# Linear attention of a two-layer decoder: the output projection as three products of parts, over two pairs of heads at a time

## The chip, the cores and the metric

The kernel runs on one core of a Trainium2 chip. The metric is the device time of one execution in microseconds, lower is better. Before the change three runs took 2131.28 to 2137.3 us, median 2136.52.

## The reference

The whole kernel is a decoder of two layers on x, 2 x 512 tokens of 512 features (1024 rows): mixer, cross attention, experts, then linear attention, gated cross attention and an MX feed-forward, each added to x after a layer norm. The change touches the fourth, linear attention (32 heads of 64 features, 16 pairs of heads):

```python
qkv = silu(h @ qkv_w.T)                       # h: normed x; q, k, v of 32 heads x 64
aw = einsum('bhid,bhjd->bhij', qi, ki) * dd   # per block, with decay
intra = einsum('bhij,bhjd->bhid', aw, vi)
inter = einsum('bhid,bhde->bhie', qi * qd_, state)
new_state = state * bd_ + einsum('bhsd,bhse->bhde', ki * kd_, vi)
attn = rmsnorm(intra + inter, norm_w)         # over all 2048 features
gate = sigmoid(h @ gate_w.T)
x = x + (gate * attn) @ out_w.T               # 1024 x 2048 by 2048 x 512
```

## The kernel before, in words

The stage is `linear_attention` (lines 1294 to 1799). Each engine has its own program, written out by hand; they meet only at semaphores, and every engine works strictly in its order. After the layer norm there is a loop over `PAIRS` = 16 pairs of heads, grouped by `GP` = 4. Tokens are 1024 in eight tiles of 128 (`TT`), in two halves of 512 (`BANK`); `CH` = 4 chunks of 128 per half.

**Parts.** An operand in F32 is split as high = rounded to F32R (ScalarE, a Copy) and low = operand - high (VectorE). `product_of_parts` (lines 227 to 231) multiplies high x high, high x low and low x high into one PSUM bank. The projections (weights `w3`, line 1457) and the values (`wv`, line 1477) go this way already. The output projection, `sum_outputs` (lines 1537 to 1546), is a plain F32 product, which the chip runs as two instructions.

**TensorE**, per pair p (lines 1551 to 1566): q.k products of the first half (line 1492), turning of the keys (1503), one projection of pair p + 1, q.k of the second half, three more projections, state updates (1513), two gate projections, outputs (1529 and 1533, PSUM banks 6 and 7). At the end of a group of four pairs come the values of the next group (eight tiles, banks 0 and 1) and then `sum_outputs(g)`: for each of eight token tiles four products, over the group's four pairs, into bank 2 or 3. These two banks are also those of q.k.

**ScalarE** (lines 1624 to 1637): moves the projections out of PSUM with Silu or Sigmoid (`pair(p + 1)`; a table load of 1.28 us stands between the two functions), makes the high parts of the weights (1611), squares the outputs (1604), at a group's end moves the values (1597); after the last pair it makes the high parts of four context tensors for the next stage (1637).

**VectorE** (lines 1780 to 1798): masks q.k (1707), decays the keys (1716), rounds the feed-forward's weights in units of two steps that have nothing to do with this stage (`round_weights`), makes low parts of weights (1767, 1772), computes the states S (1730, 1732), gates the outputs (`gate`, 1745: the normed weight times PSUM times the sigmoid, into `ga`), and at a group's end rounds two more units and adds the projection's tiles to y (`add_outputs`, 1760 and 1762). In the last one the low parts of the context tensors (1751) stand between the adds.

**GpSimd** (lines 1643 to 1659): per pair, decays the queries into `qD` (1650) and sums the squares (1659).

**SyncE** issues all transfers, also in a fixed order (lines 1407 to 1448): per pair the three projection weights, mask and query decay, stores of rounded feed-forward weights and reloads of the slot (`FSLOTS` = 4 slots in `fw`), every fourth pair the values' weights and the output weights `wo` of four pairs (1 MB). Before several of these it waits for the engine that frees the buffer.

`ga` holds five pairs (`GA`). The next stage starts after a barrier behind the last add.

## Time and profile before

| | us |
|---|---|
| median of three runs | 2136.52 |
| the profiled execution | 2135.23 |
| its span | 2133.4 |
| PE busy (share of the span) | 1935.3 (91%) |
| DVE / ACT / POOL busy | 1168.6 / 635.2 / 219.6 |
| the stage's loop in the span, about | 968 to 1576 |

PE is TensorE, DVE VectorE, ACT ScalarE, POOL GpSimd, SP SyncE; times in rows are microseconds from the span's start, unless ns. A row of the timeline has the start, the time it took, the engine, the line of the kernel, the operation, output <- inputs and how many instructions were merged; in brackets the idle time of that engine before it and what ended that. A matmul's own time includes its way through the array, so the distance between starts is what one costs. L229 to L231 are the three lines of `product_of_parts`.

### The profile page before, as it was taken

How to read it: one execution, taken by the hardware profiler on the slowest of the kernel's cores; microseconds unless marked ns; L12 is line 12 of the kernel's file. 1: busy time of each engine (PE TensorE's matmuls, PEld its weight loads, DVE VectorE, ACT ScalarE, POOL GpSimd, SP SyncE). 2: the span in 40 equal slices, each digit the busy share in tenths (PEclk: the TensorE clock that was granted, in tenths of full speed). 3: DMA queues.
4: the chain of work that ended last, by engine and by line, in shares of the span. 5: the costliest groups of instructions: out<-in, count | busy, mean ns of one | idle time of the engine just before them, and what ended most of it. 6: DMA issues, size and time to landing. Idle time of an engine off the chain costs nothing. (4 is left out here: it accounts for less than half of the span.)

```text
span 2133.4 us, 24875 instructions
## 1 busy us (share of the span) xinstructions
PE 1935.3 (91%) x9621; PEld 1409.3 (66%) x9624; DVE 1168.6 (55%) x2069; ACT 635.2 (30%) x1013; POOL 219.6 (10%) x185
## 2 busy tenths in 40 slices
PE   7899795899997599979999999999899998899996
PEld 6677783444433458847886886877758744688885
DVE  5412737555543345547674684665643378656653
ACT  3311322444444055514340331322224221222110
POOL 0000001111201100000120120210200001112221
PEclk9999896899998599999999999999999999999998
DMA  5100402222210500014221313203202100110101
GB/s 198 40 1 0 158 11 67 67 68 58 64 37 1 158 0 1 1 36 140 77 79 66 114 54 116 97 20 117 80 31 70 60 20 22 58 37 25 39 1 40
DMA packets 67125, 124.12 MB, mean 58 GB/s; under 512 B 8512, under 2 KB 26944, under 8 KB 65472
## 3 DMA queue, kind: packets, MB, share of 16 engines
q1 hardware_dynamic: 67008, 122.53, 18.1%
q8 instruction: 77, 1.26, 0.2%
q14 instruction: 40, 0.33, 0.0%
HBM read 88.82 MB, written 14.68 MB: 49 GB/s over the span
## 5 line engine op out<-in xcount | busy, mean ns | idle before, releaser
L941 DVE TENSOR_REDUCE b_nm<-ps 128x1 f32<-128x1024 f32 x128 | 151.5, 1220 | 118.8 <-PE ps L862 118.8
L929 ACT ACTIVATE b_pr<-ps 128x512 f32<-128x512 f32 x256 | 132.3, 605 | 159.5 <-PE ps L880 159.5
L229 PE MATMUL ps<-d_x_high,d_w_high 128*128 128x512 f32 x384 | 154.8, 403 | 4.4 <-DVE d_w_low L1767 4.4
L230 PE MATMUL ps<-d_x_low,d_w_high 128*128 128x512 f32 x384 | 150.4, 392 | 0.0
L231 PE MATMUL ps<-d_x_high,d_w_low 128*128 128x512 f32 x384 | 150.3, 392 | 0.0
L892 PE MATMUL ps<-b_pr,b_VS 128*64 128x512 f32 x512 | 130.6, 634 | 0.0
L1544 PE MATMUL ps<-d_wo,d_ga 128*128 128x512 f32 x256 | 110.6, 593 | 1.5 <-DVE d_ga L1745 1.5
L880 PE MATMUL ps<-b_qS,b_kS 98*128 98x512 f32 x256 | 92.3, 442 | 20.1 <-DMA b_qS<-b_nm_parts 17.7
L862 PE MATMUL ps<-b_kS,b_qS 96*128 96x512 f32 x256 | 95.0, 461 | 15.6 <-DMA b_qS<-b_q_parts 10.1
L880 PEld LDWEIGHTS ps<-b_qS,b_kS 98*128 98x128 f32 x256 | 44.1, 192 | 90.7 <-issue 52.1
L1659 POOL TENSOR_TENSOR d_sqsum<-d_sqsum,d_sq 128x512 f32<-128x512 f32 x32 | 42.4, 1325 | 487.4 <-ACT d_sq L1604 487.2
L1544 PEld LDWEIGHTS ps<-d_wo,d_ga 128*128 128x128 f32 x256 | 48.6, 190 | 61.3 <-issue 59.3
L229 PEld LDWEIGHTS ps<-d_x_high,d_w_high 128*128 128x128 f32 x384 | 72.5, 189 | 20.2 <-DVE d_w_low L1767 4.7
L231 PEld LDWEIGHTS ps<-d_x_high,d_w_low 128*128 128x128 f32 x384 | 72.5, 189 | 15.6
L230 PEld LDWEIGHTS ps<-d_x_low,d_w_high 128*128 128x128 f32 x384 | 72.7, 189 | 13.7
L862 PEld LDWEIGHTS ps<-b_kS,b_qS 96*128 96x128 f32 x256 | 53.4, 217 | 36.0 <-DVE b_nm L941 17.0
L892 PEld LDWEIGHTS ps<-b_pr,b_VS 128*64 128x64 f32 x512 | 32.9, 144 | 60.4 <-issue 51.8
L1228 DVE TENSOR_TENSOR c_hF<-ps,c_sq 128x512 f32<-128x512 f32 x64 | 44.3, 692 | 48.6 <-ACT c_sq L1216 48.6
L2333 ACT ACTIVATE f_hF_high<-ps 128x512 fp32r<-128x512 f32 x32 | 19.1, 598 | 158.2 <-PE ps L2220 158.2
L1707 DVE TENSOR_TENSOR d_A<-ps,d_mask 128x512 f32<-128x512 f32 x64 | 41.1, 684 | 36.1 <-issue 31.6
L93 POOL TENSOR_TENSOR rstd<-var_eps,neg_half 128x8 f32<-128x8 f32 x5 | 8.2, 1644 | 508.6 <-DVE var_eps L106 508.6
L1198 PEld LDWEIGHTS ps<-c_r2T,c_hF 128*128 128x128 f32 x512 | 59.5, 192 | 1.2
(372 smaller groups left out, 4592.5 us busy)
## 6 DMA issues: line engine op xcount, KB each, us to landing
b_kS<-b_k_parts SPq DMA_DIRECT2D x96, 128.0 KB, 2.3
f_rows<-d_fw SPq DMA_DIRECT2D x24, 512.0 KB, 3.0
f_w<-f_rows SPq DMA_DIRECT2D x12, 1024.0 KB, 4.8
b_qS<-b_q_parts SPq DMA_DIRECT2D x96, 64.0 KB, 2.0
a_convT<-in_convT SPq DMA_DIRECT2D x4, 1024.0 KB, 12.8
b_ctxT<-in_ctxT SPq DMA_DIRECT2D x8, 512.0 KB, 5.1
d_w<-in_d_wq SPq DMA_DIRECT2D x16, 256.0 KB, 4.4
d_w<-in_d_wk SPq DMA_DIRECT2D x16, 256.0 KB, 4.3
```

The lines of the kernel that those rows point to most:

```text
L229: nc.tensor.matmul(out, lhsT[0], rhs[0], start=start, stop=False)
L230: nc.tensor.matmul(out, lhsT[0], rhs[1], start=False, stop=False)
L231: return nc.tensor.matmul(out, lhsT[1], rhs[0], start=False, stop=stop)
L862: last = nc.tensor.matmul(c.ps[:, banks + n, :], qS[0:96, s_, h, t * P:(t + 1) * P], kS[0:96, s_, h, n * BANK:(n + 1) * BANK], start=True, ...
L880: nc.tensor.matmul(c.ps[:, 4 + n % BANKS, :], kS[0:98, g % 2, h, k * P:(k + 1) * P], qS[0:98, g % 2, h, :], start=True, stop=True).then_in ...
L892: last = nc.tensor.matmul(c.ps[2 * DH * hh:2 * DH * (hh + 1), 7, :], VS[:, 2 * (q % 2) + hh, k * VW:k * VW + VPAD], pr[:, (n + hh) % RING, :],
L929: nc.scalar.activation(pr[:, n % RING, :], c.ps[:, 4 + n % BANKS, :], ACT.Exp).then_inc(exp_done, 1)
L941: nc.vector.tensor_reduce(nm[:, g % 2, u:u + 1], c.ps[:, banks:banks + 2, :], AX.XY, ALU.max, negate=True).then_inc(job_read, 1)
L1198: last = nc.tensor.matmul(c.ps[:, 4 + n, i * LAT:(i + 1) * LAT], hF[:, e % 2, k, t * P:(t + 1) * P], r2T[:, e, k, :], start=k == 0, stop=k ...
L1228: nc.vector.tensor_tensor(hF[:, e % 2, m, n * BANK:(n + 1) * BANK], c.ps[:, 2 + j % 2, :], sq[:, j % 2, :], ALU.mult).then_inc(h_done, 1)
L1544: last = nc.tensor.matmul(c.ps[:, 2 + j % 2, :], ga[:, (g * GP + k) % GA, t * P:(t + 1) * P], wo[:, k, :], start=k == 0, stop=k == GP - 1)
L1659: nc.gpsimd.tensor_tensor(sqsum[:, tok], sqsum[:, tok], sq[:, b, :], ALU.add).then_inc(sqsum_done, 1)
```

## The change

The output projection is computed with `product_of_parts` from high and low parts of the gated outputs and of its weights. It is summed over two pairs (`SG` = 2, eight sums) instead of four. Sum i is done in the middle of pair 2i + 2, between that pair's second and third projection for the next pair, the last one at the end. ScalarE makes high parts of each pair's gated outputs after its squares and, every second pair, of the output weights (512 KB now, one buffer whose low part is written in place); VectorE makes the low parts between the key decay and the second mask product of the next pair, and adds the sum's tiles behind that mask product. SyncE loads output weights at every even round of its queue, after waiting for the sum two pairs back. `ga` shrinks to two pairs, its parts hold two, and the slots of the raw feed-forward weights go from four to three.

```diff
--- before.py
+++ after.py
@@ -1312,22 +1312,25 @@
     wv_parts = [take("wv_high", [P, KD, DM], F32R, 8), c.at("d_wv_low", [P, KD, DM], F32R, at - 16)]
     w3 = take("w3", [P, 3, KD, P], F32, 6)
     w3_parts = [take(f"w3_{part}", [P, 3, KD, P], F32R, 6) for part in ("high", "low")]
-    wo = take("wo", [P, GP, DM], F32, 8)
+    SG = 2
+    SUMS = PAIRS // SG
+    wo = take("wo", [P, SG, DM], F32, 4)
+    wo_parts = [take("wo_high", [P, SG, DM], F32R, 4), c.at("d_wo_low", [P, SG, DM], F32R, at - 8)]
     x_parts = [c.at("d_x_high", [P, KD, TOK], F32R, 16), take("x_low", [P, KD, TOK], F32R, 16)]
     v = take("v", [P, TT, DM], F32, 16)
     qF = take("qF", [P, TOK], F32, 4)
     qD = take("qD", [P, TOK], F32, 4)
     kF = take("kF", [P, TOK], F32, 4)
     kT = take("kT", [P, TT, P], F32, 4)
-    GA = GP + 1
-    ga = take("ga", [P, GA, TOK], F32, 4 * GA)
+    ga = take("ga", [P, 2, TOK], F32, 8)
+    ga_parts = [take(f"ga_{part}", [P, SG, TOK], F32R, 8) for part in ("high", "low")]
     A = take("A", [P, 2, 2, CH, P], F32, 8)
     S = take("S", [P, CH - 1, 2, P], F32, 3)
     sq = take("sq", [P, 2, BANK], F32, 4)
     sqsum = take("sqsum", [P, TOK], F32, 4)
-    FR, FSLOTS = 2, 4
+    FR, FSLOTS = 2, 3
     FUNITS = len(FJOBS) * KD // FR
-    fw = take("fw", [P, FSLOTS, FR * BANK], F32, 16)
+    fw = take("fw", [P, FSLOTS, FR * BANK], F32, 12)
     faux = take("faux", [P, FR * BANK], F32, 4)
     fscale = take("fscale", [P, FR * BANK // MX], F32, 0.125)
     finv = take("finv", [P, FR * BANK // MX], F32, 0.125)
@@ -1350,6 +1353,7 @@
     t_done, t_moved = c.sem("d_t_done"), c.sem("d_t_moved")
     u_done, s_ready = c.sem("d_u_done"), c.sem("d_s_ready")
     o_done, sq_done, ga_done = c.sem("d_o_done"), c.sem("d_sq_done"), c.sem("d_ga_done")
+    ga_high, ga_low, wo_high, wo_low = (c.sem(f"d_{n}") for n in ("ga_high", "ga_low", "wo_high", "wo_low"))
     qd_done, sqsum_done = c.sem("d_qd_done"), c.sem("d_sqsum_done")
     step, zeroed = c.sem("d_step"), c.sem("d_zeroed")
     in_cw, in_cx, c_high, c_low = (c.sem(f"d_{n}") for n in ("in_cw", "in_cx", "c_high", "c_low"))
@@ -1364,7 +1368,11 @@
 
     def a_jobs(p):
 
-        return 4 * p + TT * (p // GP)
+        return 4 * p + TT * (max(p - 1, 0) // SG)
+
+    def sum_job(i):
+
+        return 4 * min(SG * (i + 1) + 1, PAIRS) + TT * i
 
     def pair_weights(sp, p):
         for i, name in enumerate(("d_wq", "d_wk", "d_wg")):
@@ -1386,6 +1394,11 @@
     def units_rounded(p):
 
         return UNITS_FIRST + p + UNITS_GROUP * (p // GP) if p >= 0 else 0
+
+    def output_weights(sp, i):
+        if i >= 1:
+            sp.wait_ge(a_done, sum_job(i - 1) + TT)
+        sp.dma_start(wo[:], tiled(c.dram["d_woT"])[:, SG * i:SG * (i + 1), :]).then_inc(in_o, 16)
 
     def group_values(sp, g):
         sp.dma_start(wv[:], tiled(c.dram["d_wvT"])[:, :, g * DM:(g + 1) * DM]).then_inc(in_v, 16)
@@ -1407,6 +1420,8 @@
             for p in range(PAIRS):
                 if p >= 1:
                     pair_weights(sp, p)
+                if p % SG == 0 and p > SG:
+                    output_weights(sp, p // SG - 1)
                 if p >= 3:
                     sp.wait_ge(a_moved, a_jobs(p - 3) + 4)
                     sp.wait_ge(qd_done, 2 * (p - 2))
@@ -1427,11 +1442,8 @@
                         sp.wait_ge(proj_done, first_job(GP * (g - 1)) + 6 + TT)
                         group_values(sp, g)
                     if g == 0:
-                        sp.dma_start(wo[:], tiled(c.dram["d_woT"])[:, 0:GP, :]).then_inc(in_o, 16)
-                if p % GP == 1 and p > 1:
-                    g = p // GP
-                    sp.wait_ge(a_moved, a_jobs(GP * g))
-                    sp.dma_start(wo[:], tiled(c.dram["d_woT"])[:, g * GP:(g + 1) * GP, :]).then_inc(in_o, 16)
+                        output_weights(sp, 0)
+            output_weights(sp, SUMS - 1)
             sp.wait_ge(proj_done, first_job(PAIRS - 1) + 6)
             sp.dma_start(ctx.wkT[:], tiled(c.dram["e_wkT"])).then_inc(in_cw, 16)
             sp.dma_start(ctx.ctxT[:, 0], tiled(c.dram["ctxT"])[:, :, 0:CHUNK]).then_inc(in_cx, 16)
@@ -1534,15 +1546,16 @@
                                                     A[:, b, hh, ch, :], start=ch == 0, stop=True, skip_group_check=True)
                     last.then_inc(o_done, 1)
 
-            def sum_outputs(g):
-                pe.wait_ge(ga_done, 2 * GP * (g + 1))
-                pe.wait_ge(in_o, 16 * (g + 1))
+            def sum_outputs(i):
+                pe.wait_ge(wo_low, i + 1)
                 for t in range(TT):
-                    j = a_jobs(GP * (g + 1)) - TT + t
+                    j = sum_job(i) + t
+                    if t % CH == 0:
+                        pe.wait_ge(ga_low, 2 * (SG * (i + 1) - 1) + t // CH + 1)
                     pe.wait_ge(a_moved, j - 1)
-                    for k in range(GP):
-                        last = nc.tensor.matmul(c.ps[:, 2 + j % 2, :], ga[:, (g * GP + k) % GA, t * P:(t + 1) * P], wo[:, k, :],
-                                                start=k == 0, stop=k == GP - 1)
+                    for k in range(SG):
+                        last = product_of_parts(nc, c.ps[:, 2 + j % 2, :], [x[:, k, t * P:(t + 1) * P] for x in ga_parts],
+                                                [w[:, k, :] for w in wo_parts], k == 0, k == SG - 1)
                     last.then_inc(a_done, 1)
 
             queries_keys(0, 0, 4)
@@ -1555,15 +1568,18 @@
                     queries_keys(p + 1, 0, 1)
                 products(p, 1)
                 if p + 1 < PAIRS:
-                    queries_keys(p + 1, 1, 4)
+                    queries_keys(p + 1, 1, 2)
+                if p % SG == 0 and p > 0:
+                    sum_outputs(p // SG - 1)
+                if p + 1 < PAIRS:
+                    queries_keys(p + 1, 2, 4)
                 updates(p)
                 if p + 1 < PAIRS:
                     gates(p + 1)
                 outputs(p)
                 if p + 1 < PAIRS and (p + 1) % GP == 0:
                     values((p + 1) // GP)
-                if p % GP == GP - 1:
-                    sum_outputs(p // GP)
+            sum_outputs(SUMS - 1)
 
         @block.scalar
         def _(act):
@@ -1578,13 +1594,13 @@
                         act.wait_ge(qd_done, 2 * p)
                     if i == 2 and p >= 1:
                         act.wait_ge(t_done, 2 * p)
-                    if i == 4 and p >= GA:
-                        act.wait_ge(a_done, a_jobs(GP * ((p - GA) // GP + 1)))
+                    if i == 4 and p >= 2:
+                        act.wait_ge(ga_low, 2 * (p - 1))
                     if i < 4:
                         dst = (qF, kF)[i // 2][:, tok]
                         nc.scalar.activation(dst, src, ACT.Silu).then_inc(proj_moved, 1)
                     else:
-                        nc.scalar.activation(ga[:, p % GA, tok], src, ACT.Sigmoid).then_inc(proj_moved, 1)
+                        nc.scalar.activation(ga[:, p % 2, tok], src, ACT.Sigmoid).then_inc(proj_moved, 1)
                     if i % 2 == 1 and p + 1 < PAIRS:
                         high_weights(p + 1, i // 2)
 
@@ -1602,6 +1618,20 @@
                     if p >= 1:
                         act.wait_ge(sqsum_done, 2 * (p - 1) + b + 1)
                     nc.scalar.activation(sq[:, b, :], c.ps[:, 6 + b, :], ACT.Square).then_inc(sq_done, 1)
+
+            def high_gated(p):
+                for b in range(2):
+                    tok = slice(b * BANK, (b + 1) * BANK)
+                    act.wait_ge(ga_done, 2 * p + b + 1)
+                    if b == 0 and p >= SG:
+                        act.wait_ge(a_done, sum_job(p // SG - 1) + TT)
+                    nc.scalar.activation(ga_parts[0][:, p % SG, tok], ga[:, p % 2, tok], ACT.Copy).then_inc(ga_high, 1)
+
+            def high_outputs(i):
+                act.wait_ge(in_o, 16 * (i + 1))
+                if i >= 1:
+                    act.wait_ge(a_done, sum_job(i - 1) + TT)
+                nc.scalar.activation(wo_parts[0][:], wo[:], ACT.Copy).then_inc(wo_high, 1)
 
             def high_weights(p, i):
 
@@ -1625,6 +1655,9 @@
                 if p + 1 < PAIRS:
                     pair(p + 1)
                 squares(p)
+                high_gated(p)
+                if p % SG == SG - 1:
+                    high_outputs(p // SG)
                 if p % GP == GP - 2 and p + 2 < PAIRS:
                     high_values(p // GP + 1)
                 if p + 1 < PAIRS and (p + 1) % GP == 0:
@@ -1742,8 +1775,19 @@
                 for b in range(2):
                     tok = slice(b * BANK, (b + 1) * BANK)
                     dve.wait_ge(sq_done, 2 * p + b + 1)
-                    nc.vector.scalar_tensor_tensor(ga[:, p % GA, tok], c.ps[:, 6 + b, :], nw[:, p:p + 1],
-                                                   ga[:, p % GA, tok], ALU.mult, ALU.mult).then_inc(ga_done, 1)
+                    nc.vector.scalar_tensor_tensor(ga[:, p % 2, tok], c.ps[:, 6 + b, :], nw[:, p:p + 1],
+                                                   ga[:, p % 2, tok], ALU.mult, ALU.mult).then_inc(ga_done, 1)
+
+            def low_gated(p):
+                for b in range(2):
+                    tok = slice(b * BANK, (b + 1) * BANK)
+                    dve.wait_ge(ga_high, 2 * p + b + 1)
+                    nc.vector.tensor_tensor(ga_parts[1][:, p % SG, tok], ga[:, p % 2, tok],
+                                            ga_parts[0][:, p % SG, tok].bitcast(F32), ALU.subtract).then_inc(ga_low, 1)
+
+            def low_outputs(i):
+                dve.wait_ge(wo_high, i + 1)
+                nc.vector.tensor_tensor(wo_parts[1][:], wo[:], wo_parts[0][:].bitcast(F32), ALU.subtract).then_inc(wo_low, 1)
 
             def context_low(i):
                 loaded, count, raw, parts = c_splits[i]
@@ -1754,7 +1798,7 @@
                 for t in range(TT):
                     if between and t < len(c_splits):
                         between(t)
-                    j = a_jobs(GP * (g + 1)) - TT + t
+                    j = sum_job(g) + t
                     dve.wait_ge(a_done, j + 1)
                     if g == 0:
                         nc.vector.tensor_copy(y[:, t, :], c.ps[:, 2 + j % 2, :]).then_inc(a_moved, 1)
@@ -1780,7 +1824,13 @@
             for p in range(PAIRS):
                 mask_products(p, 0)
                 decay_keys(p)
+                if p % SG == 0 and p > 0:
+                    low_outputs(p // SG - 1)
+                if p >= 1:
+                    low_gated(p - 1)
                 mask_products(p, 1)
+                if p % SG == 0 and p > 0:
+                    add_outputs(p // SG - 1)
                 if p >= 1:
                     round_weights(1)
                 low_weights(p + 2, 0)
@@ -1792,10 +1842,11 @@
                     round_weights(1)
                 low_weights(p + 2, 2)
                 gate(p)
-                if p % GP == GP - 1:
-                    if p + 1 < PAIRS:
-                        round_weights(2 * UNITS_GROUP)
-                    add_outputs(p // GP, context_low if p + 1 == PAIRS else None)
+                if p % GP == GP - 1 and p + 1 < PAIRS:
+                    round_weights(2 * UNITS_GROUP)
+            low_outputs(SUMS - 1)
+            low_gated(PAIRS - 1)
+            add_outputs(SUMS - 1, context_low)
     c.rms = sqsum, ones, ms, y
 
 
```

## Rows read from the trace of the kernel before

**Rows 1.** The page's list of engines: busy us (share of the span) x instructions.

```profile
PE 1935.3 (91%) x9621; PEld 1409.3 (66%) x9624; DVE 1168.6 (55%) x2069; ACT 635.2 (30%) x1013; POOL 219.6 (10%) x185
```

**Rows 2.** Busy time by stretch: pair 14, then pair 15; granted clock, DMA share, GB/s last.

```profile
1503.10:1527.40 24.30, 24.30 (x182) 20.51 (x180) 15.02 (x32) 7.35 (x10) 5.00 (x5) 1.00 0.07 18
...
1527.40:1546.80 19.40, 10.42 (x112) 9.36 (x108) 12.80 (x26) 2.61 (x4) 6.36 (x6) 0.82 0.57 196
```

**Rows 3.** Waits of TensorE in the stage: total us, times, longest.

```profile
PE ps L1533 <- DVE d_S L1732: 6.9, 1, 6.9
...
PE ps L1492 <- DVE d_y L1762: 1.7, 2, 0.9
...
PE ps L1492 <- DVE d_y L1760: 0.9, 1, 0.9
```

**Rows 4.** Timeline of the tail, VectorE and TensorE.

```profile
1546.02 0.75 DVE L1745 SCALAR_TENSOR_TENSOR d_ga<-ps,d_nw,d_ga 128x512 f32<-128x512 f32 x1 [1.29 <-ACT d_sq L1604]
...
1546.82 27.73 PE L1544 MATMUL ps<-d_wo,d_ga 128*128 128x512 f32 x64 [1.49 <-DVE d_ga L1745]
...
1574.59 0.69 DVE L1762 TENSOR_TENSOR d_y<-ps,d_y 128x512 f32<-128x512 f32 x1 [2.74 <-PE ps L1544]
```

**Rows 5.** Timeline, first and last of 96 products of the values.

```profile
1108.28 0.50 PE L229 MATMUL ps<-d_wv_high,d_x_high 128*128 128x512 f32 x1
...
1129.99 0.39 PE L231 MATMUL ps<-d_wv_high,d_x_low 128*128 128x512 f32 x1
```

**Rows 6.** Groups by line and form: count, busy us, mean ns, idle before.

```profile
L1611 ACT ACTIVATE d_w_high<-d_w 128x512 fp32r<-128x512 f32 x48 | 29.7, 622 | 5.1 <-DMA d_w<-in_d_wq 3.2 <-PEq L194 1.9
...
L1637 ACT ACTIVATE e_ctx_high<-e_ctxT 128x1024 fp32r<-128x1024 f32 x2 | 2.1, 1046 | 0.0
...
L1751 DVE TENSOR_TENSOR e_wk_low<-e_wkT,e_wk_high 128x2048 fp32r<-128x2048 f32 x1 | 2.3, 2291 | 1.0 <-ACT e_wk_high L1637 1.0
...
L1751 DVE TENSOR_TENSOR e_ctx_low<-e_ctxT,e_ctx_high 128x1024 fp32r<-128x1024 f32 x2 | 2.4, 1215 | 0.0
```

**Rows 7.** Line 1767's durations in ns (min/median/max); GpSimd's timeline at a group's end.

```profile
L1767 DVE TENSOR_TENSOR d_w_low<-d_w,d_w_high x48: 680/692/1770, 969.3 to 1501.2; 128x512 fp32r<-128x512 f32 x48
...
1107.55 3.16 POOL L1659 TENSOR_TENSOR d_sqsum<-d_sqsum,d_sq 128x512 f32<-128x512 f32 x2 [19.04 <-ACT d_sq L1604]
```

**Rows 8.** Timeline of pair 14, three engines.

```profile
1503.13 1.16 PE L1492 MATMUL ps<-d_qF,d_kF 64*128 64x128 f32 x16
...
1508.00 1.16 PE L1492 MATMUL ps<-d_qF,d_kF 64*128 64x128 f32 x16
...
1517.39 1.50 PE L1513 MATMUL ps<-d_v,d_kT 128*128 128x128 f32 x12
...
1505.74 1.28 DVE L1716 TENSOR_TENSOR d_kT<-ps,d_kdec 128x512 f32<-128x512 f32 x2
...
1514.20 1.28 DVE L1979 TENSOR_TENSOR d_fw<-d_fw,d_fscale 128x512 f32<-128x512 f32 x2
...
1518.93 0.61 DVE L1730 COPY d_S<-ps 64x128 f32<-64x128 f32 x2 [3.44 <-PE ps L1513]
...
1519.64 1.56 DVE L1732 SCALAR_TENSOR_TENSOR d_S<-d_S,d_bdec,ps 64x128 f32<-64x128 f32 x4
...
1505.15 2.55 POOL L1650 TENSOR_TENSOR d_qD<-d_qF,d_qdec 128x512 f32<-128x512 f32 x2
```

**Rows 9.** Timeline at the first group's end, ScalarE and VectorE.

```profile
1111.42 1.28 ACT L1597 ACT_TABLE_LOAD   x1 [2.42 <-PE ps L231]
...
1109.58 1.41 DVE L1745 SCALAR_TENSOR_TENSOR d_ga<-ps,d_nw,d_ga 128x512 f32<-128x512 f32 x2
```

**Rows 10.** SyncE's timeline, and the page's list of DMA issues (median us to landing).

```profile
1161.94 0.43 SPq L1381 DMA_DIRECT2D f_rows<-d_fw  x1
...
1181.26 0.43 SPq L1373 DMA_DIRECT2D d_w<-in_d_wq  x1
...
d_w<-in_d_wq SPq DMA_DIRECT2D x16, 256.0 KB, 4.4
```

## The prediction

> **What bounds the kernel now.** I read the profile from the whole down to the one product that is changed. The page's list of engines comes first: TensorE is busy 91% of the span and the next engine 55% [rows 1]. The table by stretches then shows an ordinary pair of heads in this stage: 24.3 us, TensorE busy through all of it, VectorE 15 us, ScalarE 7 us, GpSimd 5 us, full clock [rows 2]. So in this stage time is the number of TensorE cycles, and any other engine has room as long as it is not late at one of the hand-overs. The second row there is the last pair, which has no projections of a next pair to fill its waits: 10.4 of 19.4 us. The list of waits names TensorE's idle time: 6.9 us for the state S in that last pair, and 2.6 us in three waits for the running sum y, once at the start of each later group [rows 3].
>
> The output projection is four blocks of 64 F32 instructions (32 products of two instructions each); one takes 27.7 us [rows 4], so a product costs 0.865 us. Three of the blocks stand after the values of the next group, the fourth is the stage's tail.
>
> **The change, part by part.**
> *Three products of parts.* The values have the same shapes (128x128 stationary, 512 columns) in F32R parts. Their 96 products start at 1108.28 and the last at 1129.99 [rows 5]: 21.71/95 = 0.2285 us from one to the next. Three are 0.686 us against 0.865. One sum over two pairs has 8 x 2 x 3 = 48 of them, 11.0 us. Seven such sums stand inside pairs: 76.8 us, say, against 3 x 27.7 = 83.1 us. **-6.3 us.** The eighth is in the tail.
>
> *Waits at the group start.* The F32 block was followed directly by the products q·k, whose banks waited for y [rows 3]. Now values are followed by q·k, whose banks have been free since the pair before. **-2.6 us.**
>
> *Added work on ScalarE and VectorE, each pair.* Two high copies of 128x512 (0.62 us each) and every second pair one of 128x1024 (1.05 us) on ScalarE; two subtractions of 128x512 (0.69 us) and every second pair one of 128x1024 (1.22 us) on VectorE [rows 6, 7]. y is added eight times per two pairs in place of eight per four, at 0.69 us [rows 4]. Altogether VectorE gets 32 x 0.69 + 8 x 1.22 + 32 x 0.69 = 54 us more. VectorE has 9 us free in a pair; the even pair also grows by 11.0 us, 8 x 0.69 = 5.5 of which are adds. By share nothing is lost; the order decides.
>
> *The even pair up to the sum.* Take pair 14 [rows 8]. TensorE starts q·k at 1503.13, the second half at 1508.00; that takes 1.16 us and one projection 2.74, so the sum would start at 1511.9. VectorE ends the key decay at 1507.02 and then has the subtraction of the weights, two of the gated values and the first mask product: 1.22 + 0.65 + 0.65 + 0.65. A subtraction with both inputs in SBUF that meets a GpSimd operation is late: 0.69 us usually, 1.77 once GpSimd's sum of squares had begun at 1107.55 [rows 7]. Here GpSimd multiplies queries until 1507.70, so 0.7 us more: 1510.9. Slack 1.0 us. **0**, covered by the projection between; without that cover each microsecond counts seven times.
> The Trainium skill (SBUF — State Buffer, Who interferes with whom) says that a VectorE instruction with two SBUF inputs contends with a GpSimd instruction that reads SBUF, and that the loser blocks for the other's whole instruction; the 1.77 us agrees. By that rule the change buys TensorE time with exactly the kind of instruction that GpSimd can hold up.
>
> *The even pair behind the sum.* VectorE's last add ends 0.9 us after the sum. Then come rounding (5 us), one weight subtraction (0.7) and the states (2.2), which may start when the updates are done, 2 x 2.74 + 1.5 = 7.0 us after the sum. They end at 9.2; TensorE's outputs start at 7.0 + 2 x 2.74 = 12.4. **0**, 3 us of slack. (In pair 14 rounding ends at 1515.48, 6.3 us after the second q·k, 1.3 of which are masks; the states take from 1518.93 to 1521.2, updates 1.5 us [rows 8].)
>
> *The group's end.* ScalarE waits there, after the squares, for the gated values, then copies both halves and the weights, and the first value's activation with its table load stands behind that. VectorE's gating starts at 1109.58 and ends at 1110.99 [rows 9]; copies of 0.65 and 1.0 us bring ScalarE to 1112.65, table load and activation (1.28 + 0.60) to 1114.55. The table load was at 1111.42 before. TensorE's third tile of values needs that bank at 1108.28 + 24 x 0.2285 = 1113.76. 0.9 us with the semaphore, three times. **+2.7 us.**
>
> *The last pair.* Nothing covers VectorE here, and two subtractions (1.35 us) stand ahead of the mask products and the states. As in pair 14, GpSimd's multiplications end 0.7 us after the key decay (1507.70 and 1507.02 [rows 8]): 0.7 more. **+2.05 us.**
>
> *The tail.* Before: the second gating from 1546.02 to 1546.77, the F32 block from 1546.82, the last add over at 1575.28 [rows 4]. After: gating, second high copy (1547.4), weights' high copy (1548.4), their subtraction (1549.65), first low half (1550.3): the sum starts 3.5 us later. It is 11.0 us of TensorE, but VectorE still has to subtract four context tensors between the first four adds (2 x 2.29 + 2 x 1.22 = 7.0 us [rows 6]), the second low half 0.65 and four adds 2.6: 1560.6. Only then may tile 5 run; 5, 6 and 7 take 4.1 us and the last add 0.85: 1565.4. **-9.9 us.** After some 5 us of idle TensorE the clock may be at its 1.2 GHz level, as it was in the first part of the last pair (0.82 on average there [rows 2]); mostly hidden behind VectorE: **+0.5 us.**
>
> *SyncE's queue.* The load of the output weights now waits, in every second round of the queue, for the sum two pairs back, and behind it stand masks, the stores and reloads of the rounded weights (three slots instead of four), the values' weights and the next pair's projection weights. Longest are the rounds with three stores: before, 19.3 us from the first store to the query weights [rows 10]. These transfers would start 1.5 us after the sum, and the query weights land 1.5 + 19.3 + 4.4 (median for this load [rows 10]) = 25.2 us after it. ScalarE asks for them after the second projection of the next pair, which is one pair's length behind the sum, 24.3 us. 0.9 us late, where TensorE's next need is 2 to 3 us further. With fewer transfers beside them than in that row they should be earlier. **0.** The third slot costs VectorE at most 1 to 2 us in three pairs, inside the 3 us of slack.
>
> **Sum:** -6.3 - 2.6 + 2.7 + 2.05 - 9.9 + 0.5 = -13.6 us. The profiled execution took 2135.2 us (span 2133.4), so 2121.7; the median of the runs is 1.3 us above it: **2123 us**.
>
> **Bounds of what the trace does not show.** The pitch of the new products: 0.2267 us (a steady stretch of projections) to 0.235: 0.7 us down, 2.5 up over the 384. The wait before a sum inside a pair: 0 to 1.4 us, the latter if all three subtractions take 1.77: 3 x 1.08 - 0.7 already counted, less 1.0 of slack, some 1.5; times seven, 10 us. I take 0, since GpSimd has nothing left to do after 1507.7. The tail: 11.0 + 1.5 us if nothing were in its way, 6 us less than my figure. The group's end: 0 (ScalarE's copies finding room) to 1.5 each.
>
> **The rivals.**
> 1. *TensorE's whole saving arrives* (32 x 4 x 0.18 = 23 us and the 2.6 us): the tail is not held by VectorE and the group ends cost nothing, about 2111. Against it: VectorE's 13 us of work in the tail are there whatever TensorE does. Chance 0.08.
> 2. *The low parts come late in the middle of pairs.* The port of GpSimd and VectorE holds each subtraction; 1.4 us at seven sums: -13.6 + 9.8, about 2133. For it: one such subtraction of 1.77 us is seen. Against: only the first of the three can meet GpSimd's multiplications. Chance 0.15. This is no change by measure.
> 3. *SyncE's queue becomes the bound, and the kernel slower.* Place: the projection weights of pairs 7, 11 and 15, behind three stores and three reloads. Up to 3 us late they cost nothing; beyond that TensorE stands with ScalarE, three times. If the chain took 10 us longer than the row shows, 7 or more each, over 20 us: about 2144. It decides from 6.7 us of stall each. For it: that queue already spends its time waiting, and one slot fewer ties each reload to a store that has just been issued. Against: the computed lateness is 0.9 us. Chance 0.06.
> 4. *The products of parts do not run at 0.23 us* because weights and values are written shortly before; at 0.29 us the saving is gone. Every product of parts in the trace has the same pitch. 0.02.
>
> Forecast, with its bounds (2116 to 2130): 0.69.
>
> **How the numbers follow.** A measurement of this kernel tells 0.3% (6.4 us) from nothing. Range 2112 to 2134: it takes in the forecast's bounds and rival 2, and leaves out rival 3 and most of rival 1. Faster by over 0.3% means under 2130.1: the forecast, rival 1 and the better half of rival 2, 0.80; within 0.3%: 0.13; slower: 0.07.
>
> **What would show it.** Right: sums of 48 products, 11 us each, with no wait of TensorE ahead of seven of them; no wait for y at q·k; a gap of about 0.9 us in the values at three places; the wait for S in the last pair at about 9 us instead of 6.9; in the tail about 5 us of idle TensorE, then tiles spaced by VectorE's adds and subtractions, the stage's end some 10 us nearer to the last pair's outputs. Wrong: a wait of TensorE for the low parts (of gated values or of the weights) in pairs 2 to 14, subtractions of 1.8 us there, ScalarE waiting for the projection weights of pairs 7, 11, 15, or VectorE waiting for raw rows.

## The result, and the profile after

The changed kernel takes 2119.79 us (median of 7 runs, 2116.55 to 2125.48) against 2136.52 (2130.99 to 2140.37, 7 runs): ratio 0.9929, 95% interval 0.9912 to 0.9946. That is 17 us by the medians; 2123 was predicted, in a range of 2112 to 2134.

The profiled execution of the changed kernel is its slowest run, 2125.48 us with a span of 2123.7. Its stage began 1.6 us later than in the profile of before. Over all the traces of this study that start lies between 1005.2 and 1011.6 us, behind stages that no kernel here changes. So I compare one stretch in every trace: from the stage's first q·k to the end of the last add, here called the loop (the 968 to 1576 us of the table of before take in the projections ahead of it). It is 565.3 us before (1010.01 to 1575.28) and 551.8 after (1011.59 to 1563.43): **13.4 us less, where the sum of the prediction gave 13.6**. A second trace of the unaltered changed kernel (e1 below) has 549.7; up to the states of pair 15 it agrees with the first (522.65 us in both), so the 2 us between them are in the tail. The span itself is only 9.7 us shorter: besides the 1.6 us of the later start, what stands behind the loop took 560.3 us against 558.1. The 17 us by the medians are thus more than the loop gives; the second set of runs (e1) has 11.5.

The page's list of engines, after:

```profile
PE 1918.0 (90%) x9752; PEld 1435.1 (68%) x9752; DVE 1226.4 (58%) x2141; ACT 661.2 (31%) x1053; POOL 219.6 (10%) x185
```

VectorE got 57.8 us of work (54 predicted, [rows 1] has it before) and is still far from being the bound. TensorE's busy time fell by 17.3 us. It has more instructions than before, since an F32 product counts as two and three products of parts count as three.

Waits of TensorE in the stage, after (total us, times, longest):

```profile
PE ps L1545 <- DVE d_S L1765: 8.5, 1, 8.5
PE ps L229 <- DVE d_wo_low L1790: 5.0, 1, 5.0
...
PE ps L229 <- ACT d_v L1613: 1.6, 3, 0.5
...
```

Beside [rows 3]: the three waits of q·k for y are gone, the wait for S in the last pair is 1.6 us longer, the tail has its 5 us of idle TensorE, the values have three short waits for ScalarE, and the last sum one of 0.9 us for y. What is not there counts most: no low part is waited for in front of the seven sums inside pairs. The middle of the first even pair with a sum, pair 2, VectorE, GpSimd and TensorE:

```profile
1063.19 2.55 POOL L1683 TENSOR_TENSOR d_qD<-d_qF,d_qdec 128x512 f32<-128x512 f32 x2
...
1064.96 1.85 DVE L1790 TENSOR_TENSOR d_wo_low<-d_wo,d_wo_high 128x1024 fp32r<-128x1024 f32 x1
...
1066.74 1.28 DVE L1785 TENSOR_TENSOR d_ga_low<-d_ga,d_ga_high 128x512 fp32r<-128x512 f32 x2
...
1067.95 1.28 DVE L1740 TENSOR_TENSOR d_A<-ps,d_mask 128x512 f32<-128x512 f32 x2
...
1069.98 0.39 PE L229 MATMUL ps<-d_wo_high,d_ga_high 128*128 128x512 f32 x1
```

The weights' subtraction takes 1.85 us here, beside GpSimd's multiplications, where the same form took 1.22 on its own [rows 6]: the 0.7 us extra of the prediction was 0.63. The low parts are ready at 1068.0 and the first mask product at about 1068.6, 1.4 us before the sum's first product. GpSimd holds up the weights' part in pairs 2, 6, 10 and 14 only; in pairs 4, 8 and 12 it took 1.22 us.

A second reading concerns the three values' waits. The list above says 1.6 us. The groups by line and form, restricted to the stage, have the weight loads (PEld) of the same products, count, busy, mean, then idle time and who ended it:

```profile
L229 PEld LDWEIGHTS ps<-d_wv_high,d_x_high 128*128 128x128 f32 x128 | 24.0, 188 | 8.2 <-ACT d_v L1613 2.8 <-issue 0.5
```

It is the weight load that waits, 0.93 us each time; the matmul in front covers part of it, and the PE row shows only the rest. The states S of pair 3 and of pair 4, before and then after, say the same:

```profile
1099.73 0.61 DVE L1730 COPY d_S<-ps 64x128 f32<-64x128 f32 x2 [2.84 <-PE ps L1513]
...
1174.53 0.61 DVE L1730 COPY d_S<-ps 64x128 f32<-64x128 f32 x2 [2.84 <-PE ps L1513]
```

```profile
1112.19 0.61 DVE L1763 COPY d_S<-ps 64x128 f32<-64x128 f32 x2 [2.84 <-PE ps L1525]
...
1170.31 0.61 DVE L1763 COPY d_S<-ps 64x128 f32<-64x128 f32 x2 [0.53 <-PE ps L1525]
```

It is 58.12 us after and 74.80 before. The difference is made of 27.62 (the F32 block, 1130.22 to 1157.84) and 0.88 (the wait for y) less, and 10.89 (a sum inside a pair) and 0.93 more; nothing is left over.

### The profile page after: what moved, and what is told of

The parts are those of the page before. It is cut to its first block and busy times, and to the rows that moved or that the text cites. A ratio compares the mean times of both kernels' runs of the same rounds, so it can differ in the third digit from the quotient of the medians.

```text
span 2123.7 us, 25285 instructions
## 1 busy us (share of the span) xinstructions
PE 1918.0 (90%) x9752; PEld 1435.1 (68%) x9752; DVE 1226.4 (58%) x2141; ACT 661.2 (31%) x1053; POOL 219.6 (10%) x185
## 3 DMA queue, kind: packets, MB, share of 16 engines
q8 instruction: 78, 1.28, 0.3%
## 5 line engine op out<-in xcount | busy, mean ns | idle before, releaser
L1806 DVE TENSOR_TENSOR d_y<-ps,d_y 128x512 f32<-128x512 f32 x56 | 38.7, 691 | 47.1 <-PE ps L231 47.1
L1601 ACT ACTIVATE d_kF<-ps 128x512 f32<-128x512 f32 x32 | 19.1, 598 | 135.4 <-PE ps L231 135.4
L1198 PE MATMUL ps<-c_r2T,c_hF 128*128 128x128 f32 x512 | 59.5, 275 | 0.0
```

The costliest lines, as they stand in the source:

```text
L1198: last = nc.tensor.matmul(c.ps[:, 4 + n, i * LAT:(i + 1) * LAT], hF[:, e % 2, k, t * P:(t + 1) * P], r2T[:, e, k, :], start=k == 0, stop=k ...
```

## The experiments

All are edits of the changed kernel, except e11. Ratios are to the kernel before. Loops come from one trace each, and the two traces of the changed kernel differ by 2 us.

**e1, the changed kernel again**, unaltered, for the scatter and as the baseline.

> The changed kernel once more, unaltered, for a second trace. In the first trace the loop of the stage, from the first q·k product to the last add of y, was 13.4 us shorter than before, the span 9.7 us shorter, and the medians 16.7 us apart. Theory: the change is worth the 13.4 us of its own stage, and the rest is scatter in stages that it doesn't touch (a start 1.6 us later, a wait of 2.5 us more in the feed-forward). Then the loop is again 551.8 us within 0.5 us, and the ratio is 0.9937, within 0.9915 to 0.9950. Rival: something outside the stage is faster with it; then the loop's 13.4 us explain less than the difference of the medians and another stretch of this trace is 2 us or more shorter than before.

2121.14 us (5 runs), ratio 0.9943 (0.9931 to 0.9956), loop 549.7. Two sets agree; the gain is 0.6 to 0.7%. The expected loop, 551.8 within 0.5, was missed by 2.1 us, all of it in the tail. No other stage is 2 us or more shorter than before, so the rival fell: behind the loop this trace has 559.9 us, before 558.1.

**e2, the new place without the parts.** The sums stand inside the pairs, over two pairs, but as plain F32 products; copies and subtractions are left out, and `ga` holds four pairs, since the products now read it directly.

```diff
-                        last = product_of_parts(nc, c.ps[:, 2 + j % 2, :], [x[:, k, t * P:(t + 1) * P] for x in ga_parts],
-                                                [w[:, k, :] for w in wo_parts], k == 0, k == SG - 1)
+                        last = nc.tensor.matmul(c.ps[:, 2 + j % 2, :], ga[:, (SG * i + k) % 4, t * P:(t + 1) * P], wo[:, k, :],
+                                                start=k == 0, stop=k == SG - 1)
```

> The sums stay where the change put them, over two pairs in the middle of the next pair, but are plain F32 products: no high and low parts of gated outputs or output weights. Theory: three products of parts take 0.68 us where F32 takes 0.865, so seven sums of 13.8 us instead of 10.9 cost 20.6 us more inside pairs; the tail loses the 3.5 us of parts made late and has 13.8 us of TensorE that VectorE's 12 us of work roughly match; the last pair loses the two subtractions (1.6 us) and the values their wait (1.6 us). Loop: 551.8 + 20.6 - 1.6 - 1.6 - 2 = 567 us, some 2133 to 2137 us in all, within 4 us of the kernel before. Rival: most of the gain comes from placing the sum in the middle (no wait for y, a short tail) and not from the parts; then this kernel is as fast as the changed one, about 2120 us.

2133.72 us, ratio 1.0004 (0.9994 to 1.0014), loop 564.1. The place alone gives nothing that the runs can tell. The wait for S is 6.9 us as before; the waits for y at q·k are gone, and two waits, together 2.7 us, stand in the last sum instead. The gain is that of the parts: 14.4 us between this loop and that of e1, 12.6 between the medians.

**e3, the parts without the new place.** Each sum stands directly behind the outputs of its second pair, the high and low parts just ahead of it.

```diff
-                if p % SG == 0 and p > 0:
-                    sum_outputs(p // SG - 1)
...
+                if p % SG == SG - 1:
+                    sum_outputs(p // SG)
```

> Products of parts over two pairs as in the change, but each sum stands right behind the second pair's outputs (behind the values at a group's end) and not in the middle of the next pair; the parts are made just ahead of it. Theory: the middle of the pair hides the making of the parts. Without it four sums wait as the tail does, 5 us each, three at a group's end wait some 2 us behind VectorE's rounding, and each is followed by a wait for y of 0.9 us: 20 + 6 + 6 = 32 us more than the changed kernel, about 2150 us, slower than before. Rival: the sums would find the parts ready anyway, or the clock and queue make the place of no matter: within 6 us of 2120.

2158.42 us, ratio 1.0127 (1.0111 to 1.0142), 37 us over e1; loop 590.5, 41 us over that of e1 (the trace is the slowest of the four runs). TensorE's waits:

```profile
PE ps L229 <- issue: 24.3, 4, 6.1
...
PE ps L1504 <- DVE d_y L1805: 5.3, 6, 0.9
```

The four sums that no values stand in front of wait 6.1 us each. The profile names nobody for it, but the timeline has the chain gate, high copies, the weights' low part, and then the first gated low part, which ends at 1067.19 and took 1.74 us beside GpSimd; the first sum starts at 1067.30. And q·k waits for y again. These waits are 29.6 us. The rest is behind them: after one of the four, the granted clock is the lower level for a while (windows of 4 us, clock in the column before the last two), and the products of the four sums take 1.5 to 2.8 us longer than the 10.65 us from first to last product in e1:

```profile
1066.00:1070.00 4.00, 2.70 (x7) 2.15 (x8) 1.80 (x2) 0.00 (x0) 0.65 (x1) 0.50 0.02 4
1070.00:1074.00 4.00, 4.00 (x15) 3.23 (x14) 1.50 (x3) 0.00 (x0) 0.00 (x0) 0.75 0.00 0
```

So the parts bring the gain, and something has to stand in front of each sum that covers the making of its parts. The three sums behind the values have that here too, and cost only 1.0 us each more than in e1 (59.13 us from the states of pair 3 to those of pair 4, against 58.12). The old place itself, one sum over four pairs behind the values, was not run with parts; that the middle of a pair is the only place that keeps the gain is therefore not shown.

**e4, one projection less in front of each sum**, to measure the slack that the prediction put at 1.0 us.

```diff
-                if p + 1 < PAIRS:
-                    queries_keys(p + 1, 1, 2)
                 if p % SG == 0 and p > 0:
                     sum_outputs(p // SG - 1)
                 if p + 1 < PAIRS:
-                    queries_keys(p + 1, 2, 4)
+                    queries_keys(p + 1, 1, 4)
```

> The sum in the middle of a pair stands one projection earlier, directly behind the second half of q·k. The trace of the changed kernel shows VectorE's second mask product 1.5 us ahead of the sum's start in pair 2; a projection is 2.74 us. Theory: the slack is 1.5 us and one projection is the cover, so each of the seven sums now waits 1.2 us or a little more for its banks and for the low parts (ends of the weights' subtraction and the gated values), 8 to 10 us in all. Rival: parts are ready far earlier than the order of VectorE suggests: no wait, no change.

One run, 2128.83 us; loop 559.7, 10.0 over e1.

```profile
PE ps L229 <- DVE d_A L1738: 9.1, 7, 1.6
```

2.74 us of cover taken away. The waits are 1.58 us in pairs 2, 6, 10 and 14 and 0.92 in pairs 4, 8 and 12: 1.2 us of slack where GpSimd holds up the weights' part, 1.8 where it doesn't. The releaser is the mask product, not a low part. The sum shares banks 2 and 3 with q·k, and the mask product that empties them stands behind the subtractions on VectorE. The prediction had its end as the last of the row of instructions; the name of the wait it looked for ("low parts") was not the right one.

**e5, the last pair's subtractions behind the states.** In pair 15 no sum follows in mid-pair, so the parts of pair 14 need not be early.

```diff
-                if p >= 1:
+                if p >= 1 and p + 1 < PAIRS:
                     low_gated(p - 1)
                 mask_products(p, 1)
...
                 states(p)
+                if p + 1 == PAIRS:
+                    low_gated(p - 1)
```

> Only in the last pair: the two subtractions of pair 14's gated values stand behind the states instead of ahead of the second mask product, where VectorE later waits 4 us for the squares anyway. Theory: these two are what lengthened TensorE's wait for the states from 6.9 to 8.5 us; the wait is 6.9 again, and from the first q·k of the stage to the states of pair 15 it is 521.1 instead of 522.7 us. Rival: the 1.6 us come from GpSimd or from the late sum of pair 14; the wait stays 8.5.

One run, 2116.26 us; the wait for S is 6.9 us again, as before the change, and from the first q·k to the states of pair 15 it is 521.0 us in place of 522.65, which shows that the 1.6 us are these two subtractions. The whole loop, 549.3, doesn't tell 1.6 us from the scatter of the tail.

**e6, the weights' parts a pair earlier**, high at the end of the even pair, low ahead of the odd pair's states.

```diff
-                if p % SG == SG - 1:
+                if p % SG == 0:
                     high_outputs(p // SG)
...
+                if p % SG == SG - 1:
+                    low_outputs(p // SG)
                 states(p)
```

> The parts of the output weights are made one pair earlier: the high part on ScalarE at the end of every even pair, the low part on VectorE ahead of the states of every odd pair, where it waits 2.8 us for the updates. Theory: at a group's end ScalarE is 1.05 us earlier at the values and TensorE's three waits there (1.6 us) go; in the tail the chain outputs - square - gating - high - low loses the copy and the subtraction of the weights, TensorE waits 2.1 us instead of 5.0, but the stage ends only some 1.5 us sooner, since VectorE's context subtractions then wait for ScalarE's copies. 3 to 4 us in all, about 2117. Rival: the tail is TensorE's own chain; then it ends the whole 2.9 us sooner and the kernel gains 4.5. Second rival: the sums inside pairs were held by the weights' subtraction; then the distance of the states from pair 1 to pair 2 (35.24 us) shrinks.

2114.91 us, ratio 0.9916 (0.9891 to 0.9942), loop 547.3.

The values wait no more, and the tail's wait falls from 5.0 to 2.6 us. The wait for S grows by 1.2, to 9.7 us: in pair 15 the weights' subtraction stands ahead of the states, which I had overlooked.

**e7, two of the context splits in the last pair**, so that VectorE has 3.5 us less between the adds of the last sum. ScalarE makes their high parts ahead of its squares.

```diff
                 low_weights(p + 2, 2)
+                if p + 1 == PAIRS:
+                    context_low(0)
+                    context_low(1)
                 gate(p)
...
-                    if between and t < len(c_splits):
-                        between(t)
+                    if between and 1 <= t <= 2:
+                        between(t + 1)
```

> Two of the four context tensors are split in the last pair, while ScalarE and VectorE wait for the outputs, and the other two between the first adds of the last sum. Theory: VectorE's 13 us of work hold the tail; without 3.5 of them TensorE's 10.9 us hold it, the adds follow every 1.36 us, and the stage ends 2 to 4 us sooner (the clock's level decides how much), about 2117. Rival: the tail is held by TensorE's low clock after its 5 us of waiting, not by VectorE; then the same end.

2121.15 us, ratio 0.9936 (0.9916 to 0.9957), loop 549.4 against 549.7. The theory fell, in this kernel: the last sum, from its first product to the end of the last add, takes 14.6 us against 15.0 in e1. What is left standing is the lower clock, which e9 tests.

**e8, the three edits together** (e5, e6, e7, with the weights' last low part ahead of the states as in e6).

```diff
                 if p % SG == SG - 1:
                     low_outputs(p // SG)
                 states(p)
+                if p + 1 == PAIRS:
+                    low_gated(p - 1)
...
+                if p + 1 == PAIRS:
+                    context_low(0)
+                    context_low(1)
                 gate(p)
```

> The three edits together: pair 14's low parts behind the states of pair 15, the output weights' parts a pair earlier, two context tensors in the last pair. Theory: they add up, since each takes work from another place of one chain, the tail then being TensorE's own 10.9 us behind a wait of 2.1 us: 1.6 + 1.6 + 2.9 and some 2 of the adds, less 0.7 because VectorE's idle 4.1 us before the gating are a little too short for all that is put there: 7 to 9 us less than the changed kernel, about 2112. Rival: once one is gone the next wait takes its place; 3 to 4 us.

2111.46 us (2110.66 to 2112.18), ratio **0.9893** (0.9874 to 0.9912), loop 545.1. This is the fastest kernel of the study: 21 us under the runs of the kernel before in its own set (2132.32), and 8 to 10 under the change as made, of which its loop shows 4.6 to 6.7. Its wait for S is 8.1 us, that of the tail 2.6.

**e9, keeping TensorE busy while it waits.** Spare F32 products into a bank that nothing reads, eight between the last pair's updates and outputs, five ahead of the last sum; the splits are where the change has them.

```diff
+            def spare(count):
+                pe.wait_ge(proj_moved, first_job(PAIRS - 1) + 6)
+                for _ in range(count):
+                    nc.tensor.matmul(c.ps[:, 0, :], kT[:, 0, :], v[:, 0, :], start=True, stop=True)
...
+                    spare(8)
                 outputs(p)
...
+            spare(5)
             sum_outputs(SUMS - 1)
```

> The changed kernel with spare F32 products on TensorE into a bank that nothing reads: eight between the last pair's state updates and its outputs (6.9 us at 0.865 each, inside the 8.5 us of waiting), five between those outputs and the last sum (4.3 us inside the 5.0). They compute nothing that is used. Theory (the rest of the tail's loss is the lower level of the clock after TensorE has stood idle): the last pair's outputs take about 3.3 us in place of 4.8 to 5.2, the first products of the last sum come 0.68 us apart per three instead of 1.28, and the loop is 546.5 to 547.5 us instead of 549.7 to 551.8. Rival A (VectorE's adds and subtractions hold the last sum whatever the clock is): only the outputs gain, 1.5 us, loop about 548.5, last sum's length unchanged at about 14.6 us. Rival B (the spare products delay what they precede): loop not below 550.

2118.83 us, ratio 0.9923 (0.9905 to 0.9942), loop 547.9. In e1 the wait and the outputs, then the start of the last sum:

```profile
1532.00:1536.00 4.00, 0.00 (x0) 0.00 (x0) 3.70 (x10) 0.00 (x0) 0.00 (x0) 0.53 0.81 319
1536.00:1540.00 4.00, 3.92 (x46) 3.93 (x48) 0.02 (x1) 0.60 (x1) 0.00 (x0) 0.61 0.01 4
...
1545.80:1549.00 3.20, 3.19 (x8) 2.53 (x9) 3.07 (x3) 3.20 (x3) 0.00 (x0) 0.52 0.00 0
```

and in e9, outputs and start of the sum:

```profile
1530.00:1534.00 4.00, 3.38 (x57) 3.21 (x58) 1.28 (x3) 0.66 (x2) 0.91 (x1) 1.00 0.13 52
...
1539.00:1543.00 4.00, 3.65 (x15) 2.69 (x16) 4.00 (x4) 3.43 (x3) 0.00 (x0) 1.00 0.00 0
```

The clock stays at its upper level, 2.4 GHz, and the outputs take 3.3 us in place of 4.7 (1530.62 to 1533.89; 1536.08 to 1540.81). But the last sum is 14.7 us long, where e1 had 15.0: rival A. There VectorE holds it, its instructions following one another without idle time up to 1549. If the clock and VectorE's splits are two limits of about the same size, taking away one of them, as e7 and e9 do, gains little; e12 tests both together.

**e10, the wait for S taken on as well.** Over e8: the second half of a rounding unit moves from pair 15 to pair 14, the weights' low part goes behind the states, three splits stay in the sum and one is early. The line of the rounding:

```diff
-                    round_weights(1)
+                    round_weights(2 if p + 2 == PAIRS else 1)
```

> All three edits of the tail as in e8, and the last pair's wait for the states S taken on: two units of the feed-forward's rounding go to the end of pair 14 and none stands ahead of the states in pair 15; the gated parts and the weights' low part for the sum in that pair are made behind the states; of the context splits only the first comes early, the others stay between the first adds of the last sum. Theory (in the last pair TensorE waits for VectorE's row of instructions, of which 1.9 us of subtractions, 1.5 of the weights' and some 2.5 of rounding now go away from before the states): wait for S about 8.1 - 5 = 3 us, loop 545.1 - 3 to 4 = 541.5, about 2108 us by the median. Rival (the rounding moved to pair 14 delays that pair's gated values, TensorE then waits at the next q.k or in the last sum but one): the wait for S falls, but another of the same size comes in pair 15, loop about 545.

2114.93 us, ratio 0.9908 (0.9892 to 0.9925), loop 546.5: the rival was right.

```profile
PE ps L1504 <- DVE d_A L1747: 7.4, 2, 6.6
```

The wait for S fell from 8.1 to 2.4 us, and 6.6 us came up at q·k. The rounding delays pair 14's gate, behind which the mask product stands, and it also became slower itself: VectorE and GpSimd in that stretch,

```profile
1516.54 3.37 POOL L1690 TENSOR_TENSOR d_qD<-d_qF,d_qdec 128x512 f32<-128x512 f32 x2
1517.05 3.41 DVE L2041 TENSOR_TENSOR d_fw<-d_fw,d_fscale 128x512 f32<-128x512 f32 x2
```

The two VectorE instructions take 1.28 us on their own [rows 8], GpSimd's 2.55.

**e11, the kernel before with three slots** for the raw feed-forward weights.

```diff
-    FR, FSLOTS = 2, 4
+    FR, FSLOTS = 2, 3
```

> The kernel before with one edit: three slots for the feed-forward's raw weights in place of four. Theory (the third slot costs nothing, as the prediction had it: SyncE waits, nobody waits for SyncE): no change, ratio within 0.998 to 1.002, no new wait of TensorE in the stage. Rival (a reload tied to a store just issued makes VectorE wait for raw rows, 1 to 2 us in three pairs, and TensorE with it): 3 to 6 us slower, ratio about 1.002.

2134.53 us (10 runs), ratio 1.0 (0.9991 to 1.0009), loop 565.5, TensorE's waits those of before. In the old order of the queue the slot costs nothing, and VectorE waits for no raw rows.

**e12, e10 with spare products**, three and two.

```diff
+                    spare(3)
                 outputs(p)
...
+            spare(2)
             sum_outputs(SUMS - 1)
```

> The kernel of e10 with spare products as in e9, three before the last pair's outputs (2.6 us) and two before the last sum (1.7 us). Theory (clock): outputs of the last pair at full clock, 1.5 us less, and up to 1 us less in the last sum: loop about 539.5, 2106 us. Rival (the waits that are left are too short to lower the clock, so that spare products can only be in the way): the same as e10 or up to 1 us slower.

2114.52 us, ratio 0.991 (0.9893 to 0.9926), loop 545.3, 1.2 less than e10, where up to 2.5 were expected; e10 and e12 can't be told apart by their times. Outputs and sum run at full clock, and the last sum takes 13.5 us. The four cases side by side, first product to end of the last add: 15.0 (e1), 14.7 (e9, full clock), 14.7 (e10, one split early), 13.5 (e12, both). With two splits early at the lower clock it is 14.6 (e7) and 14.3 (e8). These are single traces, and a last sum that nothing was done to takes 15.0 to 15.7 us in six of them (the change, e1, e3, e4, e5, e6), so 14.7 hardly differs from those and 13.5 does. 48 products 0.227 apart and 0.9 us up to the end of the add would be 11.8; two splits still stand between the first three adds. The outputs of e12 are 1.7 us shorter than in e10, but the sum starts no sooner (10.0 us behind the start of the states in both): the early split stands ahead of the gating on VectorE and ends 1.2 us after the outputs.

## Why the prediction was right

*The parts' pace.* Predicted 0.2285 us a product, 11.0 us a sum. The seven even pairs are 10.89 us longer than the others (pair 1 to 2: 35.24 between the starts of S, against 24.35 to an odd pair), so 7 x 10.89 = 76.2 us replace three blocks of 27.62: -6.6, predicted -6.3. e2 confirms that this is where the gain is.

*Waits for y.* Gone, -2.6, as predicted; e3 brings them back when q·k follows a sum directly.

*The group's end.* 2.8 us in three, predicted 2.7; e6 takes them away.

*Together up to pair 15.* -6.6 - 2.6 + 2.8 = -6.4, predicted -6.2; the trace has -6.5: three boundaries of -16.68 (58.12 for 74.80) and four even pairs of +10.89.

*The last pair.* +1.6 on TensorE, predicted 2.05. The 0.7 us of meeting GpSimd was 0.59 (1.87 us for two subtractions of 1.28 together), and some 0.2 us in front of the mask product had been idle before; e5 shows the cause.

*The tail.* From the start of the last states to the end of the last add 37.6 us before, 29.2 after (27.1 in e1): -8.5 and -10.6, predicted -9.4. The sum starts 4.3 us later in the first trace and 2.9 in the second (from the start of S 13.46 and 12.05 us, 9.18 before), predicted 3.5: the chain to the sum's first product is those 3.5 us, a wait of 5.0 for 1.5, and the rest is the length of the outputs at one clock or the other (6.1 and 4.7 us, 5.4 before); from its first product to the end of the last add it takes 15.7 and 15.0 us, predicted 15.1. So the size was right; that it falls between the two is in part luck, since they are 2 us apart. One reading behind it was incomplete: that the lower clock is "mostly hidden behind VectorE". In the last sum either of the two alone costs about as much as both: e9 and e10 each take one away for 0.3 us, which is within the scatter, e12 both for 1.5. In the outputs ahead of the sum nothing hides the clock, 1.5 us in e9. The place of the lower clock before was misread, too: of the last pair it is not the first part, which is TensorE at full clock and then waiting, but the outputs behind the wait:

```profile
1540.00:1544.20 4.20, 4.20 (x40) 4.20 (x42) 0.22 (x1) 0.60 (x1) 0.28 (x1) 0.50 0.15 60
```

*In the middle of even pairs.* Slack of 1.0 us predicted for pair 14, 1.2 measured there (e4). Behind the sum 3 us predicted; the states end 3.1 us before the outputs. The direction of rival 2 was real: one projection less in front of the sum costs 10 us of the 13.4. Only its size was not enough. The Trainium skill (SBUF — State Buffer, Who interferes with whom) says that a VectorE instruction with two SBUF inputs and a GpSimd instruction that reads SBUF contend; the trace agrees, with 1.85 us for 1.22. In odd pairs, which have no weights' part, it is a subtraction of gated values that is hit (mean of all 32 0.84 us, median 0.68), with no sum behind it.

*SyncE.* Its queue waits 217 us in total for the sums, and TensorE does not wait for it:

```profile
SPq L1401 <- PE ps L231: 217.2, 7, 41.1
```

A wait there costs nothing while no consumer stands behind it. ScalarE and TensorE have no wait for the projection weights of pairs 7, 11 and 15. One of the signs of being wrong did show, though: VectorE waits for raw rows once, in pair 4,

```profile
1174.47 1.28 DVE L1997 TENSOR_REDUCE d_fscale<-d_fw 128x16 f32<-128x512 f32 x2 [1.10 <-DMA d_fw<-in_f_u]
```

1.1 us here, 0.5 in e1, and not at all before or in e11. It is of the size that the prediction allowed, and no wait of TensorE follows from it: from the states of pair 4 to those of pair 5 it is 24.35 us, as before. Rival 3 had no part in the time.

*The chances.* They don't add up as stated: the forecast, rival 1 and half of rival 2 are 0.69 + 0.08 + 0.075 = 0.845, not 0.80.

What stays open: the 2 us between the two traces of the changed kernel are in the tail, where the clock rose at a different moment; why, no run here shows. Nor do they show why the stage's start varies by 6 us; the granted clock over the first 1000 us is 0.91 in the traces that start it at 1007 us or later, before among them, and 0.92 in those that start it sooner.

## What to carry to other kernels

Where TensorE is the bound, replacing an F32 product by three products of parts pays 0.18 us for each 512 columns here, but only if the splitting work stands where another engine's slack hides it: with the chain directly in front of four of the eight sums the same arithmetic lost 1.3%. When a stage's end may be held by two things of like size, test them together before calling either harmless. And before moving work out of the way of one wait, list what stands behind it in its new place: in e10 the wait moved, and in e6 a part of it did.

## What I had not expected of the hardware

A wait of TensorE also costs after it has ended. Behind 8.5 idle us the outputs took 4.7 us (e1), and with spare products in that gap 3.3 (e9); behind the 6.1 us waits of e3 three products took 1.28 us instead of 0.68 for some 3 to 5 us. VectorE and GpSimd, running F32 instructions on SBUF at the same time, can both be slower for several instructions on end: some 1.7 us each in e10, four of VectorE and two of GpSimd, where alone they take 0.64 and 1.27.
